# Constant products that nobody reads, placed on TensorE around the linear attention of a two-layer decoder

## What is computed

```python
x = x + L0_attn(layernorm(x))        # rotary self-attention, 16 heads
x = x + L0_xattn(layernorm(x), ctx)  # attention-free transformer on the context
x = x + L0_ffn(layernorm(x))         # 8 linear experts, top 2
x = x + L1_attn(layernorm(x))        # linear attention: softmaxed q, k, and their complements, times sin and cos
x = x + L1_xattn(layernorm(x), ctx)  # causal masked attention on the context, 16 heads
x = x + L1_ffn(layernorm(x))         # 4 experts with gelu, top 2, 4 rounds
```

## Time and profile before

| what | us |
|---|---|
| median of 3 runs | 507.46 |
| lowest and highest of them | 506.75, 507.61 |
| the profiled execution's own time | 509.59 |
| its span, first to last instruction | 507.9 |
| PE busy | 443.4 |
| DVE busy | 345.4 |
| ACT busy | 308.4 |
| POOL busy | 144.5 |

### The profile page before, as it was taken

How to read it: one execution, slowest core, us unless ns; L and a number is a source line. 1 busy time by engine, 2 the same in 40 slices (tenths; PEclk the granted TensorE clock), 3 DMA queues, 4 the chain that set the end, 5 groups by cost and what they waited for, 6 DMA issues and landing times.

```text
span 507.9 us, 8227 instructions
## 1 busy us (share of the span) xinstructions
PE 443.4 (87%) x2660; PEld 340.5 (67%) x2660; DVE 345.4 (68%) x943; ACT 308.4 (61%) x603; POOL 144.5 (28%) x210
## 2 busy tenths in 40 slices
PE   1898999978983898579899797999999999999994
PEld 1576777747731686447777665687878787878783
DVE  3567777696379575557777767858676776768663
ACT  1577677541255433035666466877787878787881
POOL 7282201222065100034644431222222222222222
PEclk9999999998797899859999999999999999999998
DMA  8214441000400000001111002020202112020201
GB/s 298 66 39 143 128 140 31 1 1 1 166 1 0 1 1 1 0 9 33 35 30 25 23 1 83 0 86 0 84 1 85 32 52 82 1 83 1 85 1 41
DMA packets 14053, 24.03 MB, mean 47 GB/s; under 512 B 4000, under 2 KB 10784, under 8 KB 12608
## 3 DMA queue, kind: packets, MB, share of 16 engines
q1 hardware_dynamic: 13584, 22.71, 13.9%
q10 hardware_dynamic: 432, 0.85, 0.4%
HBM read 19.29 MB, written 0.59 MB: 39 GB/s over the span
## 4 chain that ended last, share of the span: by engine, by line
PE 34%; issue 7%; DVE 6%; POOL 2%; ACT 2%; DMA 1%; SPq 0%; POOLq 0%; DVEq 0%
PE ps L1662 5%; PE ps L1664 4%; PE ps L1663 4%; PE ps L1697 4%; PE ps L1698 4%; PE ps L1696 4%; POOL xnT L502 2%; DVE masked L911 2%; PE ps L1372 2%; PE ps L1329 2%; PE ps L1339 1%; PE ps L1639 1%; DVE odif L946 1%; ACT bigr L763 1%; PE ps L1384 1%
## 5 line engine op out<-in xcount | busy, mean ns | idle before, releaser
L1163 DVE TENSOR_TENSOR bigr<-ps,bigr 128x512 fp32r<-128x512 f32 x128 | 86.1, 689 | 51.6 <-ACT ps L764 51.6
L763 ACT ACTIVATE bigr<-ps,b 128x512 fp32r<-128x512 f32 x128 | 89.9, 702 | 32.3 <-PE ps L1664 32.3
L626 ACT ACTIVATE big<-ps 128x512 f32<-128x512 f32 (+1 forms) x128 | 69.0, 550 | 47.8 <-PE ps L1339 46.2
L764 ACT ACTIVATE ps<-ps,b 128x512 f32<-128x512 f32 x128 | 86.7, 678 | 0.0
L502 POOL TENSOR_TENSOR xnT<-xnT,big 128x512 f32<-128x512 f32 x32 | 41.4, 1293 | 148.7 <-DVE big L1171 148.7
L1329 PE MATMUL ps<-bigr,qk 128*128 128x256 f32 (+1 forms) x256 | 62.5, 331 | 7.4 <-DVE nmax L918 2.7
L1662 PE MATMUL ps<-k1hi,w1hi 128*128 128x512 f32 x128 | 52.8, 412 | 2.7 <-DVE bigr L1163 2.2
L1329 PEld LDWEIGHTS ps<-bigr,qk 128*128 128x128 f32 x256 | 40.3, 195 | 21.6 <-issue 12.8
L918 DVE TENSOR_REDUCE nmax<-ps 128x2 f32<-128x512 f32 x64 | 42.7, 688 | 17.3 <-PE ps L1329 16.8
L1696 PE MATMUL ps<-bigr,w2hi 128*128 128x512 f32 x128 | 51.1, 399 | 0.0
L1664 PE MATMUL ps<-k1lo,w1hi 128*128 128x512 f32 x128 | 50.6, 396 | 0.0
(11 more groups left out here) (194 smaller groups left out, 800.9 us busy)
## 6 DMA issues: line engine op xcount, KB each, us to landing
big<-gates SPq DMA_DIRECT2D x8, 1024.0 KB, 4.6
bigr<-qk SPq DMA_DIRECT2D x112, 32.0 KB, 1.8
wi<-in_wi SPq DMA_DIRECT2D x4, 512.0 KB, 4.3
wo<-in_wo SPq DMA_DIRECT2D x4, 512.0 KB, 4.5
big<-in_sel SPq DMA_DIRECT2D x1, 1024.0 KB, 8.7
wo<-in_w SPq DMA_DIRECT2D x1, 1024.0 KB, 4.8
wi<-in_w SPq DMA_DIRECT2D x1, 1024.0 KB, 7.0
x<-in_x SPq DMA_DIRECT2D x1, 512.0 KB, 4.8
```

The lines of the kernel that those rows point to most:

```text
L626: act.activation(prob[:, h % 8, c], ps[:, 2 + h % 2, c], ACT.Exp, scale=DH ** -0.5).then_inc(s(L + "_exp"), 1)
L763: act.activation(ghi[:, u % 2, c, :], ps[:, c, :], ACT.Gelu_apprx_tanh, bias=b1[:, u % E1, c:c + 1])
L764: act.activation(ps[:, c, :], ps[:, c, :], ACT.Gelu_apprx_tanh, bias=b1[:, u % E1, c:c + 1]).then_inc(s("ff1_gel"), 1)
L1163: v.tensor_tensor(glo[:, u % 2, c, :], ps[:, c, :], ghi[:, u % 2, c, :].bitcast(f32), ALU.subtract).then_inc(s("ff1_glo"), 1)
```

## The change

A helper on PE issues products of `ident` with all 512 columns of `turn` into a given PSUM bank. Nothing reads them; the bank is written again by the next real work before anyone reads it. The helper waits for nothing and signals nothing. It is called at five places: 16 products after the waits that precede `at1`'s first transposes, 8 products before `xa1`'s first transposes, 2 between these and the query projection, 5 between the query projection and the first stacks, and 3 between the first stacks and the first scores. Nothing is removed, and no other engine's program is touched.

```diff
+            def keep_busy(count, bank):
+
+                for _ in range(count):
+                    pe.matmul(ps[:, bank, :], ident[:, :], turn[:, :, :, :].rearrange("p t z n -> p (t z n)"),
+                              start=True, stop=True)
+
...
             pe.wait_ge(s("ld_at1"), 8 * 16)
             pe.wait_ge(s("zeroed"), 2)
+            keep_busy(16, 5)
             transpose_xn("at1", 0, QT)
...
+            keep_busy(8, 1)
             transpose_xn("xa1", 0, 6)
+            keep_busy(2, 1)
             query_projection(0, 0)
+            keep_busy(5, 1)
             cur = xnT
...
-            attention("xa1", True, k1hi[:, :], k1lo[:, :], {0: (s("xa1_lo"), 1), 2: (s("xa1_lo"), 2)}, lambda: None,
+            attention("xa1", True, k1hi[:, :], k1lo[:, :], {0: (s("xa1_lo"), 1), 2: (s("xa1_lo"), 2)}, lambda: keep_busy(3, 1),
```

## The result

The changed kernel takes 517.10 us (median of 4 runs, 515.54 to 517.68) against 507.11 for the one before; the ratio is 1.0172, 95% interval 1.0148 to 1.0197. The two medians are 10.0 us apart. The ratio on record is an estimate of its own and not their quotient, which would be 1.0197, the upper end of its interval; by the ratio the loss is 8.7 us (7.5 to 10.0). The forecast was 516.5, 9.0 more, and lies between the two.

What follows compares the result with a forecast made beforehand. The prediction took one chain through PE to bound both entries, its lateness paid in full unless the faster clock gave it back. 3.3 + 5.7 = 9.0 us on 507.46 made 516.5 us, range 513.0 to 521.5.

Steps and rivals of the forecast that it cites:

- The price of a product: On PE, one float32 product of 512 columns takes 0.86 us; 34 take 29.2 us against 13.4 us of idle time.
- The rule for bf16 products: Skill's pace for PE, columns divided by 2.4 GHz, 0.216 us for 512; weighed, but the float32 row's 0.86 preferred.
- Into `at1`: Linear attention's entry: transposes 5.6 us late, 2.2 given back by the clock, so 3.3 us later; the rest unchanged.
- Into `xa1`: Masked attention's entry: 7.35 us late, less 0.2 and 1.45 given back, net 5.7 us later.
- the delay: Masked attention's entry: PE's chain starts the first scores at 230.5 in place of 223.19, 7.35 us late.
- what is given back in the first eight heads: Masked attention: most of DVE's idling for PE at low clock goes, 1.45 us taken, bounds 0 and 1.75.
- The clock: PE stays at 1.00 through both entries, with the first projection at some 1.96 us rather than 3.64.
- rival 2: Both entries: products, nearly all zeros, don't hold the clock; about 545 us; chance 0.07.
- Rival 1: Both entries: products take 0.23 us and fit the gaps, so the kernel is faster, 502 to 504 us; chance 0.05.
- Rival 3: Both entries: another chain, later than PE's, covers the delay; within 0.2%, about 507.5 us; chance 0.05.
- The sum: Whole kernel: 3.3 + 5.7 = 9.0 us more, median 516.5 us, 1.8% slower.

Runs made afterwards that it cites:

- at1_double: Changed kernel with 32 products instead of 16 ahead of the linear attention and none elsewhere; ratio to the kernel before 1.0339, 17.2 us more.
- tuned: Changed kernel with long products only where they fit (9, 2, 3), short float32r ones in small gaps and first heads; 0.9895 of before, 5.3 us less.
- one_pass: Changed kernel with the same counts, each product from float32r constants (0.23 us instead of 0.86); 0.9956 of before, 2.2 us less.
- fitted: Changed kernel with counts cut to fit the idle times: 9, 3, 0, 1, 0 instead of 16, 8, 2, 5, 3; 0.9935 of before, 3.3 us less.
- late_idle: Kernel before, no products, PE made to wait for later DVE work before the linear attention's first transposes; 1.0065 of before, 3.3 us more.
- xa1_only: Changed kernel with only the 18 products at the masked attention's entry; 1.0120 of before, 6.1 us more.
- fitted_out: As fitted, plus 2 products before the linear attention's last transposes; 0.9933 of before, 3.4 us less.
- at1_only: Changed kernel with only the 16 products ahead of the linear attention; 1.0074 of before, 3.8 us more.

## Why the prediction was right, point by point

**The price of a product** was right: 0.86 by line 1532's row, 0.859 by at1_double. The group of the product in the page of after:

```profile
L1245 PE MATMUL ps<-turn,ident 128*128 128x512 f32 x68 | 30.1, 594 | 0.0
```

Its mean of 594 ns is the length of a record, not its pace; 68 records at 0.43 are 29.2 us. The Trainium skill ("FP8 and Floating Point Precision", "TensorE Precision Notes") has true float32 take four passes through the array. The traces agree in size: 0.86 against 0.23 is 3.7 times, though a product leaves two records and not four. The rule for bf16 products that the prediction weighed, with its 0.216 us, doesn't apply to these operands: 0.859 was measured.

**Into `at1`**: predicted 3.3, measured 17.09 - 13.81 = 3.28, with the transposes and projections at the lengths taken from the earlier trace rows. The rest of the linear attention was to stay as it was, and did within 0.2.

**Into `xa1`**: predicted 5.7, measured 3.23 + 3.99 - 0.88 = 6.3. The chain was right, link by link; two terms were mis-sized. The first is the delay. By local times (the output projection starts 0.51 later in this trace) the first scores' record starts at 230.62, predicted 230.5, but that closeness is luck: the record starts while the last of the three products is still running (the series ends at 228.85 + 2.84 = 231.69). By the pace of the series, six records 0.43 apart, PE can take the scores at about 231.43, an estimate, or 230.9 by local times, 0.4 later than predicted. Most of that, 0.3, lies in the stacks: from their start at 228.15 to the next product at 228.85 it is 0.70, where I had 0.4, because I had halved the time to the start of their last row and left out that row itself. DVE's first scores are 7.45 late by local times, predicted 7.15. (The table has 7.22 for the delay, since line 1117 came 0.23 later behind the start of the output projection than before.)

The second is what is given back in the first eight heads: of the 1.45 only 0.88 came. In tuned, with the clock at 1.00 in these heads as well, 1.38 came. The difference, 0.50, is the size of a meeting of DVE and POOL, told below, that made line 833 take 2.07 us here and 1.58 in tuned; no run isolates it.

**The clock** was at 1.00 in all of both entries, as taken, which settles rival 2 (products of near-zeros that don't hold it). **Rival 1** would have needed products of less than 0.6 us; one_pass and fitted show that its mechanism is real at another length. **Rival 3**, a covered delay, is out by late_idle, where a delay of 3.65 us lengthened the entry by 3.69.

**The sum**: 9.0 predicted; 9.75 in the trace from line 1514 on, 10.0 between the medians, 8.7 by the ratio. The profiled execution was to take 518.6 and took 516.87: the prediction took the stretch ahead of line 1514 to be as in the profile of before, and there this execution was 2.75 us faster.

## What to carry to other kernels

A filler is worth what the clock gives back and costs what hangs over its gap, and only the second is certain. Take the filler's price from a row with the same operand types and columns (here 0.86 us for float32, 0.23 for float32r), divide the gap in the trace by it, and stay below: 34 products cost 9 to 10 us, 14 long and 13 short ones, laid into the gaps, gained 5. A low clock in a profile is an opportunity only as large as the work on the path that ran in it, here about 5 us, however long the idle stretches look.

## What the hardware showed that I had not expected

The clock fell again in the first heads of fitted at 222, with PE busy for 5.80 of the following 6.00 us. What PE had done before that were the sparse steps between the query projection and the first scores. In xa1_only it fell at 234 behind the same long products behind which it stayed at 1.00 in after. Holding the clock through an entry doesn't hold it for what comes next.

Four tiles' normalisation (line 833) takes 1.09 us at 215.72 in the trace of before, beside two small operations of POOL on 128x4 (0.23 at 215.90 and 1.04 at 216.21). Beside POOL's four casts it took 1.65 there:

```profile
215.72 1.09 DVE L833 TENSOR_SCALAR xn<-x,mv,rstd 128x128 f32<-128x128 f32 x4
225.12 1.65 DVE L833 TENSOR_SCALAR xn<-x,mv,rstd 128x128 f32<-128x128 f32 x4
```

```profile
224.92 1.75 POOL L381 CAST bigr<-qk 32x256 fp32r<-32x256 f32 x4 [7.68 <-ACT qk L555]
```

In after it took 2.07, next to one POOL operation of 1.32:

```profile
233.08 2.07 DVE L833 TENSOR_SCALAR xn<-x,mv,rstd 128x128 f32<-128x128 f32 x4
```

```profile
231.22 1.75 POOL L381 CAST bigr<-qk 32x256 fp32r<-32x256 f32 x4 [13.24 <-ACT qk L555]
233.04 0.23 POOL L363 COPY vaug<-v_tok 128x64 f32<-128x64 f32 x1
233.23 1.32 POOL L448 TENSOR_TENSOR w1lo<-wo,w1hi 128x512 fp32r<-128x512 f32 x1
```

The late PE had shifted DVE against POOL: DVE's first scores came 7.96 us later than in before, POOL's casts, which wait for ACT, only 6.30. The Trainium skill ("SBUF — State Buffer", "Who interferes with whom") has a scalar operation of VectorE in a two-port mode and a GpSimd operation take turns on a shared port pair. The three durations are compatible with that, but no run here took POOL's operation away or shows the mode, so it is argued and not shown.

Stretches of low clock also come and go from one execution to the next in places that no edit touched: 118 to 140, 193 to 204 (in xa1_only, fitted, fitted_out and late_idle), 304 to 329 (in at1_only, one_pass and at1_double). Where they show in the table they are worth 1.3 to 2.5 us each, more than some of the differences measured here.
